# Moving the weighting of gathered rows, and the last norm, from VectorE to ScalarE in two stages of a graph network kernel

## The reference

```
def _spmm(edge_row, edge_col, edge_vals, Z):
    msgs = edge_vals[:, None] * Z[edge_col]
    return jax.ops.segment_sum(msgs, edge_row, num_segments=N_NODES)

x = _layernorm(x + _L0_gnn_ref(x, src, dst, edge_weight, W, b))        # [x, Z1, Z2, Z3] @ W + b, Zk = spmm(Zk-1)
x = _layernorm(x + _L1_gnn_ref(x, edge_index, edge_attr_48, ...))      # sum, max, mean of edge attributes, an MLP
x = _layernorm(x + _L2_gnn_ref(x, edge_index, Wq, bq, ...))            # attention over edges, plus x @ Wskip
x = _layernorm(x + _L3_gnn_ref(x, edge_weight, src, dst))              # (x + 3 * spmm(x)) / 4
```

## Time and profile before

| | |
|---|---|
| median of three runs | 6072.8 us (6069.09 to 6074.92) |
| profiled execution, its own time | 6074.08 us |
| its span, first to last instruction | 6072.2 us |
| mean granted TensorE clock | 0.869 |
| busy: PE, DVE, ACT, POOL | 72%, 72%, 52%, 73% |
| source stage (first gather of Z2 to the target stage's first gather) | about 2016 to 3145 us |
| last stage (first gather of X3 to the end) | about 5034 to 6072 us |

### The profile page before, as it was taken

The page is one execution under the profiler, slowest core; times in us unless marked ns, Lnnn a source line. Parts: engine busy times, 40 slices in busy tenths (PEclk is TensorE's granted clock), DMA queues, the critical chain, the costliest instruction groups (busy, mean ns, idle before and its releaser), DMA issues. The chain is left out here.

```text
span 6072.2 us, 102714 instructions
## 1 busy us (share of the span) xinstructions
PE 4362.9 (72%) x25328; PEld 3182.1 (52%) x25328; DVE 4394.4 (72%) x8168; ACT 3146.3 (52%) x6667; POOL 4430.8 (73%) x4339
## 2 busy tenths in 40 slices
PE   1059899998888799999989999888878873422200
PEld 0047688886666677777765555544444442211100
DVE  8966699997888688888865555599999995743300
ACT  0047688886666455555544444378888881110000
POOL 7777566667777777777757777577777766777777
PEclk9999999999999899999999999988888885555555
DMA  5377488886888799999977777634444438943311
GB/s 126 100 142 181 132 250 253 251 250 197 286 285 286 198 262 264 263 262 264 262 199 224 226 225 227 197 106 116 114 117 114 114 104 265 328 133 94 92 40 40
DMA packets 1005231, 1151.65 MB, mean 190 GB/s; under 512 B 184599, under 2 KB 641235, under 8 KB 1004182
## 3 DMA queue, kind: packets, MB, share of 16 engines
q1 hardware_dynamic: 831958, 834.69, 46.0%
q0 software_dynamic: 137984, 247.24, 16.8%
q10 hardware_dynamic: 35136, 68.16, 3.1%
HBM read 688.22 MB, written 523.68 MB: 200 GB/s over the span
## 5 line engine op out<-in xcount | busy, mean ns | idle before, releaser
L1008 PE MATMUL bank<-ident,gat 128*128 128x128 f32 x2352 | 423.6, 309 | 633.2 <-DVE zT L2008 558.9
L1111 PE MATMUL bank<-x1T,W1x 128*128 128x512 f32 x1568 | 764.9, 600 | 24.5 <-ACT x1T L1304 24.5
L1125 PE MATMUL bank<-W2s,hT 128*128 128x128 f32 x6272 | 777.8, 277 | 1.0 <-ACT hT L1388 1.0
L1125 PEld LDWEIGHTS bank<-W2s,hT 128*128 128x128 f32 x6272 | 734.5, 193 | 16.8 <-ACT hT L1388 1.7
L1008 PEld LDWEIGHTS bank<-ident,gat 128*128 128x128 f32 x2352 | 305.0, 161 | 760.1 <-issue 576.2
L1314 ACT ACTIVATE mbuf<-t 128x512 f32<-128x512 f32 x490 | 309.9, 633 | 581.3 <-DVE t L2042 309.3
L1388 ACT ACTIVATE hT<-bank,b1u 128x512 f32<-128x512 f32 x784 | 502.9, 679 | 183.7 <-PE bank L1111 183.4
L751 POOL DMA_INDIRECT gat<-XD,s_q x392 | 376.8, 961 | 243.1 <-ACT codes_z L1414 109.8
L1008 PE MATMUL bank<-ident,x 128*128 128x128 f32 x3136 | 481.7, 277 | 94.6 <-DVE x L1973 84.6
L751 POOL DMA_INDIRECT gat<-X,d_x x392 | 397.4, 1014 | 205.3 <-issue 205.0
L788 POOL DMA_INDIRECT VQ<-s_v,s_q x392 | 448.7, 1145 | 119.5 <-issue 117.6
(11 more groups left out here) (369 smaller groups left out, 11316.5 us busy)
## 6 DMA issues: line engine op xcount, KB each, us to landing
X<-x SPq DMA_DIRECT2D x588, 256.0 KB, 2.6
fB<-row_s_same SPq DMA_DIRECT2D x392, 256.0 KB, 5.1
Y<-x SPq DMA_DIRECT2D x294, 256.0 KB, 3.7
xT<-in_x_fm SPq DMA_DIRECT2D x196, 256.0 KB
ffB<-rows_last_notlast SPq DMA_DIRECT2D x98, 512.0 KB
out_rows<-Y ACTq DMA_DIRECT2D x28, 1792.0 KB
Z1T<-zT SPq DMA_DIRECT2D x98, 256.0 KB
Z1E<-zE SPq DMA_DIRECT2D x98, 256.0 KB
```

The lines of the kernel that those rows point to most:

```text
L1008: mm = pe.transpose(dst[:, t, :], tiles[t], ident[:, :])
L1111: mm = pe.matmul(bH[h][:, :, :], W1x[:, cols], x1T[s][:, :], start=kind != "d", stop=True)
L1125: mm = pe.matmul(bMLP[:, t, :], hT[h][s][:, t * P:(t + 1) * P], W2s[:, h, :], start=False, stop=h == HC - 1, skip_group_check=True)
```

## The change

ScalarE's `activation` with the function Copy and a scale that is one number per partition multiplies a row of 128 features by its weight. A tile has four rows per partition, so one product of VectorE becomes four scaled copies. The change does this in three places:

- In the source stage `z_weigh(2)` leaves VectorE's list and enters ScalarE's, behind `relu` and ahead of `seed_mm1`.
- In the last stage `z_weigh(3)` leaves VectorE's list and stands on ScalarE behind `copy_pieces`.
- In the last stage VectorE's `fin_norm` becomes `fin_scale`, the reciprocal alone, which counts up a new semaphore `scaled`; the product is made by four scaled copies on ScalarE (`fin_norm`), between `z_weigh(3)` and `square`.

The waits on free tiles (`fin_free`) go with the product to ScalarE. The first two weightings, in the node stage, stay on VectorE.

```
@@ AFTER
-            "att_src": ("z_rows", 2 * EI), "gathered_x": ("gathered_d", 0), ...
+            "att_src": ("z_rows", 2 * EI), "scaled": ("scale34", EI), "gathered_x": ("gathered_d", 0), ...
@@ block.scalar
+            def z_weigh(k):
+
+                def stage(i, s):
+                    c = seq(k, i)
+                    if void(act, i, s, ("weighted", c, 1)):
+                        return
+                    at(act, "gathered", s, moved(5 if k == 3 else k, i + 1, s))
+                    for t in range(T):
+                        w = bass.ds((i * SL + s) * T + t, 1)
+                        a = act.activation(gat[s][:, t, 0:P], gat[s][:, t, 0:P], ACT.Copy, scale=wts[:, w])
+                    a.then_inc(S("weighted", s), 1)
+                return stage
...
-            steps(act, EI, (square("s", 0), 1), (std("s", 0), 1), (relu("s"), 2), (seed_mm1("s"), 0), (x2_out("s"), 4),
+            steps(act, EI, (square("s", 0), 1), (std("s", 0), 1), (relu("s"), 2), (z_weigh(2), 0), (seed_mm1("s"), 0),
+                  (x2_out("s"), 4),
                   (x_src, 0), (square("s", 1), 3), (seed_mlp("s"), 2), (std("s", 1), 3), (x1_out("s"), 1), (square("s", 2), 4),
                   (std("s", 2), 4), peeled=1)
...
-            steps(act, EI, (copy_pieces, 0), (square("fin", 3), 2), (std("fin", 3), 2), unrolled=True)
+            def fin_free(i, s):
...
+            def fin_norm(i, s):
+                if void(act, i, s, ("ln4_out", x4i("fin", i), 1)):
+                    return
+                ready(act, "scaled", s, i)
+                fin_free(i, s)
+                dst = held[i][s].rearrange("p (t f) -> p t f", t=T) if i < HB else x4[s]
+                for t in range(T):
+                    a = act.activation(dst[:, t, :], t2[s][:, t, :], ACT.Copy, scale=lns[3][2][s][:, t:t + 1])
+                a.then_inc(S("ln4_out", s), 1)
+
+            all_slots(act, "agg_turned", EI)
+            steps(act, EI, (copy_pieces, 0), (z_weigh(3), 0), (fin_norm, 3), (square("fin", 3), 2), (std("fin", 3), 2),
+                  unrolled=True)
@@ block.vector
-            steps(dve, EI, (norm2("s"), 4), (z_weigh(2), 0), (power("s", 0), 1), (norm1("s"), 1), (z_scan(2), 0),
+            steps(dve, EI, (norm2("s"), 4), (power("s", 0), 1), (norm1("s"), 1), (z_scan(2), 0),
...
-            def fin_norm(i, s):
...
-            steps(dve, EI, (z_weigh(3), 0), (power("fin", 3), 3), (z_scan(3), 1), (fin_norm, 3), (fin_sum, 2), unrolled=True)
+            def fin_scale(i, s):
+                if void(dve, i, s, ("scaled", i, 1)):
+                    return
+                _, sd, rs, _ = lns[3]
+                ready(dve, "deviation3", s, i)
+                at(dve, "ln4_out", s, x4i("fin", i))
+                dve.reciprocal(rs[s][:, :], sd[s][:, :]).then_inc(S("scaled", s), 1)
+
+            steps(dve, EI, (power("fin", 3), 3), (z_scan(3), 1), (fin_scale, 3), (fin_sum, 2), unrolled=True)
```

More of the change, by code:

```diff
@@ L92, in gnn_kernel @@
             "q_out": ("x1T", NI + 2 * EI), "decay": ("relu", NI + 2 * EI), "weight": ("x2T", NI + EI),
-            "att_src": ("z_rows", 2 * EI), "gathered_x": ("gathered_d", 0), "ld_attr": ("st_xd", EI * 16),
+            "att_src": ("z_rows", 2 * EI), "scaled": ("scale34", EI), "gathered_x": ("gathered_d", 0), "ld_attr": ("st_xd", EI * 16),
         }
@@ L1475, in copy_pieces @@
                     act.dma_start(out_runs[w, :], src_runs[w, :]).then_inc(S("copied"), 16)
-            steps(act, EI, (copy_pieces, 0), (square("fin", 3), 2), (std("fin", 3), 2), unrolled=True)
+            def fin_free(i, s):
+                if i == HB - 2:
+                    at(act, "st_x3_", s, 2 * EI * 16)
+                elif i == HB:
+                    at(act, "scattered2", s, moved(1, 0, s))
+                elif i > HB:
+                    reuse(act, "scattered", s, i - HB, 64)
+            def fin_norm(i, s):
[10 more added lines that the diff above has]
+                  unrolled=True)
         @block.vector
@@ L2242, in fin_sum @@
                                          op0=ALU.mult, op1=ALU.add).then_inc(S("fin_sum", s), 1)
[L2244 to L2250, removed]
-            def fin_norm(i, s):
-                dst = [h.rearrange("p (t f) -> p t f", t=T) for h in held[i]] if i < HB else x4s
-                norm("fin", 3, lambda s: t2[s], dst, "ln4_out", fin_free)(i, s)
-            steps(dve, EI, (z_weigh(3), 0), (power("fin", 3), 3), (z_scan(3), 1), (fin_norm, 3), (fin_sum, 2), unrolled=True)
+            def fin_scale(i, s):
[6 more added lines that the diff above has]
+            steps(dve, EI, (power("fin", 3), 3), (z_scan(3), 1), (fin_scale, 3), (fin_sum, 2), unrolled=True)
 def kernel(**inputs):
```

## The result

The changed kernel takes 6388.4 us (median of 4 runs, 6383.1 to 6389.6); the kernel before took 6071.4 beside it. The ratio is 1.052, with a 95% interval of 1.0507 to 1.0534: slower by some 317 us. The forecast was 6502 us in a range from 6320 to 6590.

The account below looks back on a forecast made before the run. The prediction took the source stage's loop of VectorE, ScalarE and PE, and POOL in the last stage, as the bounds. It summed 6074 + 274 (loop) + 167 (clock) - 13 (last stage) = 6502 us, range 6320 to 6590.

Parts of the forecast that it names:

- What bounded the kernel: Source stage: the loop of VectorE, ScalarE and PE, 11.3 us per step, sets the pace; POOL, at 10.9, runs ahead.
- The loop's links: Source stage: seven links through VectorE, ScalarE and PE sum to 14.15 us; step grows by 2.8 us, 274 us in all.
- The copies' price: Source stage: four scaled copies on ScalarE take 1.3 us per group, between bounds of 1.07 and 1.63.
- The clock: Source stage: PE's clock falls in most steps, each step loses 1.7 us, 167 us in all; bounds nothing and 282.
- The last stage: Scatters from `x` no longer contend with VectorE's products: 13 us less, between -25 and +17 us.
- The sum: Whole kernel: 6074 + 274 + 167 - 13 = 6502 us.
- The other signs that were named: Changed profile: VectorE idle 2.4 us before `zT`, over 1 before `layer2`; POOL waiting; copies 1.3 us; scatters near 982 ns.
- POOL's pace: Rival, source stage: POOL's 10.9 us per group sets the step and the kernel gets faster, 6010 us; faster given 0.06.
- Half speed throughout: Rival, source stage: PE at half speed for the turns and `chain_c` in every step, 6617 us; chance 0.04.
- the full clock: Rival, source stage: the same loop, but PE's clock holds, 6335 us, range 6310 to 6430; chance 0.18.
- the forecast's own: Whole kernel: the longer loop plus a clock fall in the source stage, 6502 us, range 6430 to 6590; chance 0.70.

Follow-up runs that it names:

- e3: The changed kernel with the source stage's weighting put first in ScalarE's list, ahead of `square` and the root: 6025.6 us, ratio 0.9926 to the kernel before.
- e4: The changed kernel with the source stage's weighting moved between the root and `relu` in ScalarE's list: 6264.9 us, ratio 1.0323 to the kernel before.
- e5: The changed kernel with eight idle turns of the identity on PE in front of each source group's turns: 6285.1 us, ratio 1.0353 to the kernel before.
- e11: The changed kernel with the source stage's four copies cut into eight of 64 columns, and sixteen idle turns per group on PE: 6354.7 us, ratio 1.0457.
- e6: The changed kernel with the source stage's four weighting copies of 128 columns cut into eight of 64: 6595.3 us, ratio 1.0863 to the kernel before.

## Why the prediction was right, and where it missed

**What bounded the kernel** was read rightly: not an engine's busy share, but who waits for whom. The loop of the changed kernel has the links in the order that was given, and e3 and e4 take it apart by one entry of a list.

**The loop's links** were nearly right. In the second step shown above, with its clock at full, they come to 13.92 us, where 14.15 were forecast.

| link (start to start, us) | forecast | second step |
|---|---|---|
| `layer2` to `ln2vr` | 1.35 | 1.39 |
| to the sum `ln1vr` | 6.25 | 6.24 |
| to the root | 0.71 | 0.71 |
| root and `relu`, to the copies | 1.46 | 1.34 |
| copies, to the turn | 1.40 | 1.32 |
| turns, to `chain_c` | 0.93 | 0.93 |
| `chain_c`, to `layer2` | 2.05 | 1.99 |

The three links that were too long are those for which busy times were added up, two of them with 0.1 us on top, instead of starts subtracted from starts. ScalarE's next instruction starts 0.1 us before the last one ends (`relu` ends at 2766.40, the copies start at 2766.29), and PE and VectorE started 0.04 to 0.05 us behind the end of what they waited for, not 0.1. Over the stage the loop cost 243 us where 274 were forecast. The copies' price, 1.3 us, measured 1.27. The estimate from the Trainium skill (ScalarE: Activation LUTs, What ACT_TABLE_LOAD costs) was 1.27 as well, so the trace agrees with that section.

**The clock** is the step that failed in size. "So I expect the clock to fall in most steps" held, in 64 of 92; that "the step loses 1.7 us" in all 98 did not. A step with the fall is 1.4 us longer than one without (15.26 against 13.87), and three in ten have none. The term is 89 us instead of 167, and the granted clock of the stage 0.92, not the 0.85 that was named as its sign. The error was to take the length of one fall in the attention stage for that of every step here. The measured 89 lies between the bounds that were named, nothing and 282 us. The prediction also took the 1.32 us of idle time there as enough for a fall; e5 and e11, with waits of 1.6 to 1.7 us and no fall in 92 steps each, show that such a wait need not bring one.

**The last stage** was -28 us, not -13, and below the low end of -25. The contention was the right mechanism for most of it, but the sum counted it on the scatters alone and left the gathers out, since no undisturbed gather was in the trace. The scatters gave 232 x 49 ns = 11 us, where 13 were forecast; the gathers 392 x 23 ns = 9 us; the wait at the stage's beginning, which the prediction did not have, the other 7. ScalarE's new copies there stayed under POOL's issue: POOL's waits for ScalarE's `x` come to 4.8 us.

**The sum**, term by term: 6074 + 274 + 167 - 13 forecast; 6074 + 243 + 89 - 28 measured, and 5 us of small changes, at the stage's beginning and in the stages between, gives the profiled 6383. The terms missed on the same side, so no error hid another. The other signs that were named came out: VectorE idle ahead of `zT` 2.2 us per wait (210.2 / 96; 2.4 forecast), ahead of `layer2` 1.7 (164.4 / 94; over 1), POOL waiting for the turns, copies of 1.27 us, scatters near 982.

**The rivals.** POOL's pace, the case on the other side, was rightly given little, for the reason that was named (the order of ScalarE's queue): with the order changed, e3 is faster than the kernel before, though not at POOL's pace. Half speed throughout did not come with this change, but e6, where the wait is 0.7 us longer, comes near it: its step is 17.10 - 14.61 = 2.5 us longer than that of the same copies at full clock (e11), where the rival had 2.9. The time that came lies in the range that was given to the full clock (6310 to 6430) and below the forecast's own (6430 to 6590), though the clock did fall: the cases treated the clock as the same in every step, and what happened was a mixture, 28 steps of the one kind and 64 of the other. So the range from 6320 to 6590 held because it joined two cases; the case that was given 0.70 missed with its own.

What stays open: why the clock falls behind one wait of 2.58 us and not behind the next, and behind more than half of the waits of 1.44 us in e4 but behind none of 1.71 us in e5. The granted clock and the length of `chain_c` show that it does; no run here tells on what it depends.

## What to carry to other kernels

Idle time of an in-order engine can be used only from the place in its queue at which it stands: before giving it new work, look up what ends the wait ahead of that place, and whether the work's result feeds back to it. Here the same four copies cost 345 us behind the root and saved 21 us of the stage ahead of it. Where an engine waits in a loop, put a price on its clock step by step and not as one constant, and take link lengths from start to start.

## What was not expected of the hardware

- Idle work paid: eight turns of 128 x 128 per group, 1.04 us of PE's time, made the kernel 103 us faster, since PE came out of its wait at 2.4 GHz (granted clock 1.00 instead of 0.92).
- A longer wait was dearer than its length: 0.74 us more of copies cost 2.1 us per group (207 us over 98 groups), since `chain_c` was partly at half speed in 91 of 92 steps instead of 64. But a wait of 1.44 us in e4 brought the fall in 53 of 92 steps, and one of 1.71 us in e5 in none.
- VectorE's product with both inputs in SBUF lengthens an indirect DMA instruction of POOL that begins just behind the product's start: a scatter that began 0.04 to 0.14 us behind it took 1.41 to 1.52 us instead of 0.98, while 88 others that overlapped a product took at most 1.19. Gathers are lengthened too (952 ns on average without products, 981 with two per group).
